# Norms and value copies moved to ScalarE, the output projection moved ahead of the next values, keys split around the rows' transposition: a four-layer cross-attention kernel with a mixture of experts

## The chip, the cores and the metric

The kernel runs on one core of one Trainium2 chip. The metric is the device time in microseconds (us) of one execution. Engines are named TensorE (PE in the profile, with its weight loads as PEld), VectorE (DVE), ScalarE (ACT), GpSimd (POOL) and SyncE (SP, which here only starts transfers).

## What is computed

The input is `x` (32 sequences of 128 positions, 256 wide) and a context of the same shape, all in fp32. Four layers follow each other, all with 16 heads of 16 dimensions:

```
L0: x = norm(x + attn(x -> ctx));  x = norm(x + relu(x W1) W2)         (key mask)
L1: x = norm(x + attn(x -> ctx))
L2: x = norm(x + attn(x -> x, causal) + bias);  x = norm(x + attn(x -> ctx));
    x = norm(x + top-2-of-8 mixture of experts(x))
L3: windowed attention, one shared key and value head; a silu gate;
    rms norm; the mean over the positions is subtracted
```

A layer norm is `(x - mean) * rsqrt(var + 1e-5) * g + b`. The causal attention has biases on queries, keys, values and output, and so has the cross attention of L2.

## The kernel before

The kernel has three stages. The **attention stage** (`slots`) handles L0, L1 and the two attentions of L2, which the code numbers `l` = 0 to 3. Its unit is a slot: one attention of one sequence. A round (`TPI`) is 16 slots, `tau` = 0 to 15: four layers for `NS` = 4 sequences, so `tau` 0 to 3 are `l` = 0 of four sequences, 4 to 7 are `l` = 1, and so on. Eight rounds make 128 slots; the first and last are unrolled by hand, the six between are a loop. The **expert stage** runs 71 tiles of 128 sorted rows through the experts. The **combine stage** (`cslots`, 32 slots) gathers the experts' results, norms them, and does L3.

Every engine has its own instruction stream, and the order inside a slot is written out by hand; semaphores (`wait`, `then_inc`) join the streams. An engine executes its stream in order, so whatever stands behind a waiting instruction waits too. Slot `now` is worked on together with its neighbours: `prev` (one before), `ff` (two before), `rk_` (three before), `nxt` (one after) and `nn` (two after). In a slot, in the order of each stream:

- TensorE: `scores(now)` into the four banks `ps_s`; the projections of queries and keys of `nxt` into `ps_qk` (`project_qk`); `av(prev)`, the attention-weighted values; `maxima_t`, which turns the row maxima round; `xt(nn)`, which turns the rows of `nn` round into the first half of bank `ps_xv`; `scores_t(now)`, the transposed scores minus the maxima; `values(nxt)` into the second half of `ps_xv`; `wo(prev)`, the output projection, into `ps_w`.
- VectorE: `norm_stats` (three small instructions), `maxima(now)` (L1520, one reduction over 128x2048), `norm_apply` (L1548, 128x256), `normalise(prev)` (the contexts are turned over by a 32x32 transposition out of PSUM, divided, and turned over again into `oT`, L1535), `vz_evac(nxt)` (the values are copied out of PSUM, with the bias added for `l` 2 and 3, L1489 and L1491), `qk_lo(nxt)` (the low parts of queries and keys), `residual_sum` (L1678, reads the output projection out of `ps_w`).
- ScalarE: `qk_evac(nxt)` (high parts of queries and keys out of `ps_qk`), `mt_evac` (copies the turned maxima into `mT`, which `scores_t` needs), `xt_evac(nn)`, `exps(now)` (four 128x512 exponentials), `fxt_evac` (rows for the feed-forward or the router).
- GpSimd: `root` (the inverse root of the variance, 128x1), `residual` (two 128x256 operations that need the norm's output), `expand` and `expand_lo` (queries spread over the heads), and in four slots of a round the two indirect stores of `scatter`.

The feed-forward of L0 makes slots 3 to 6 longer. A slot in which `rk_` is of layer 0 (`tau` 3 to 6) has `ff_output(rk_)` behind its scores, then `maxima_t`, `av`, for `tau` 3 to 5 `fxt(ff)`, `scores_t(now)`, `xt(nxt)` and `project(nxt)` (keys, values, queries), then `wo(prev)`; `tau` 6 has `xt(nxt)` and `project_qk` ahead of `scores_t`. Slots 2 to 5 end with `ff_hidden(ff)`, which fills `ps_xv` and `ps_qk`. VectorE applies two norms in the heavy slots, the one of `ff` and the one behind the feed-forward of `rk_`. In `tau` 14, 15, 0 and 1, `ff` is of layer 3 and `fxt(ff)` turns its rows round for the router, behind `wo`.

In the combine stage the maxima are turned round into the bank `ps_qk`, and `maxima_t` waits until the low parts of the slot after have been taken from that bank. There the norm is already applied by ScalarE (`combine_apply`, L1403), with the product of the negated mean and the inverse root made by GpSimd (`c_root`, L2103).

## Time and profile before

| | |
|---|---|
| median of 3 runs (lowest to highest) | 2236.9 us (2232.33 to 2238.15) |
| the profiled execution | 2241.2 us, span 2239.3 us |
| TensorE matmuls busy | 1964.6 us, 88% of the span |
| TensorE weight loads busy | 1664.2 us, 74% |
| VectorE busy | 1579.5 us, 71% |
| ScalarE busy | 1108.7 us, 50% |
| GpSimd busy | 1074.5 us, 48% |
| mean granted clock of TensorE | 0.972 of full speed |

The profile covers one execution. Each row below gives an instruction or a group of them with its line in the kernel (L1520 is line 1520), what it writes and reads (`out<-in`), its size and how many of them were merged. A time in square brackets is how long the engine stood still before it, and behind the arrow stands what ended that. Instructions of one engine overlap a little, so the next one can start before the one before it ends.

### The profile page before, as it was taken

Reading aid. Unit: us, or ns where it says so; the run is one execution under the profiler, and the core shown is the slowest. Engines: PE = TensorE matmul, PEld = TensorE weight load, DVE = VectorE, ACT = ScalarE, POOL = GpSimd, SP = SyncE. Lnnn points to the kernel's source line nnn. Section 1 sums busy time; section 2 is a strip of 40 time slices with the busy share of each in tenths; the row PEclk is TensorE's granted clock in tenths of the full one; section 3 lists DMA queues with packets and bytes.
Section 4 is the critical chain, followed back from the end, with each engine's and each line's share of the span. In section 5 each row is a group of like instructions: output and inputs, shape, how many; then the busy total and the mean of one; then the engine's idle time right before and its main releaser. Section 6 shows DMA issues by size and latency. Waiting matters only on the chain.

```text
span 2239.3 us, 72637 instructions
## 1 busy us (share of the span) xinstructions
PE 1964.6 (88%) x26040; PEld 1664.2 (74%) x26041; DVE 1579.5 (71%) x3469; ACT 1108.7 (50%) x2836; POOL 1074.5 (48%) x1432
## 2 busy tenths in 40 slices
PE   5988888888888888888888885999999996888887
PEld 4777777767767777777767764999999995666665
DVE  4688788787787787787787784544545454788886
ACT  2355355345354354354354442556565653566665
POOL 3455365465465464465454465140224004777874
PEclk9999999999999999999999996999999996999999
DMA  8401001001001001001000213121111112122120
GB/s 195 174 2 39 7 21 39 8 21 44 7 19 42 6 19 42 6 19 42 6 19 18 97 41 118 59 65 50 59 59 59 40 40 59 56 64 66 59 61 24
DMA packets 97540, 104.65 MB, mean 47 GB/s; under 512 B 23968, under 2 KB 88480, under 8 KB 97184
## 3 DMA queue, kind: packets, MB, share of 16 engines
q1 hardware_dynamic: 88224, 76.22, 11.4%
q0 software_dynamic: 8704, 25.19, 3.6%
q8 instruction: 167, 2.74, 0.5%
q14 instruction: 61, 0.50, 0.1%
q10 hardware_dynamic: 384, 0.01, 0.0%
HBM read 64.94 MB, written 36.44 MB: 45 GB/s over the span
## 4 chain that ended last, share of the span: by engine, by line
PE 48%; issue 20%; DVE 19%; POOL 6%; ACT 3%; DMA 1%; SPq 1%; another core or an unknown queue 1%; DVEq 1%; POOLq 0%; ACTq 0%
PE ps_scores L1106 11%; PE ps_w L1119 9%; DVE mb L1520 8%; PE ps_scores L880 5%; PE ps_xv L785 3%; PE ps_xv L707 3%; ACT pt_all L1272 3%; DVE lower L1508 3%; PE ps_scores L887 2%; PE ps_scores L860 2%; PE ps_qk L801 2%; PE ps_w L930 1%; POOL lower L1975 1%; POOL rstd L1991 1%; PE ps_scores L827 1%
## 5 line engine op out<-in xcount | busy, mean ns | idle before, releaser
L1520 DVE TENSOR_REDUCE mb<-ps_scores 128x16 bf16<-128x2048 f32 x160 | 365.8, 2286 | 57.3 <-PE ps_scores L860 56.4
L1272 ACT ACTIVATE pt_all<-ps_scores 128x512 f32<-128x512 f32 x512 | 267.1, 603 | 73.2 <-PE ps_scores L887 54.2
L1106 PEld LDWEIGHTS ps_scores<-tiles,w_now 128*128 128x128 f32 x2272 | 267.2, 193 | 4.8 <-issue 1.8
L1106 PE MATMUL ps_scores<-tiles,w_now 128*128 128x128 f32 x2272 | 267.8, 277 | 1.2 <-DVE tiles L1811 1.2
L1358 ACT ACTIVATE tiles<-ps_scores,b1s 128x128 f32<-128x128 f32 x568 | 154.2, 383 | 198.3 <-PE ps_scores L1106 182.8
L1991 POOL TENSOR_TENSOR rstd<-ve,neghalf 128x1 f32<-128x1 f32 x192 | 106.9, 557 | 280.5 <-DVE ve L1544 259.2
L1968 POOL TENSOR_TENSOR qbd_all<-qT,consts 128x512 fp32r<-128x512 f32 x160 | 177.6, 1110 | 97.9 <-ACT kT L1258 74.1
L1119 PE MATMUL ps_w<-w_split,g_split 128*128 x1136 | 219.4, 346 | 5.7 <-DVE g_split L1830 5.7
L1975 POOL TENSOR_TENSOR lower<-lower,consts 128x512 fp32r<-128x512 f32 x160 | 166.8, 1042 | 97.4 <-DVE lower L1508 63.0
L1119 PEld LDWEIGHTS ps_w<-w_split,g_split 128*128 128x128 f32 x1136 | 174.9, 190 | 30.4 <-issue 6.4
L917 PE MATMUL ps_o<-pt_all,vz 128*32 128x128 f32 x5120 | 175.4, 278 | 0.0
L1821 DVE TENSOR_TENSOR tiles<-ps_w,tiles 128x256 f32<-128x256 f32 x71 | 30.2, 425 | 186.8 <-PE ps_w L1119 186.8
L1243 ACT ACTIVATE xT<-ps_xv,cols_all 128x128 f32<-128x128 f32 x256 | 103.2, 453 | 115.2 <-PE ps_xv L707 114.2
L1996 POOL TENSOR_TENSOR xr<-xn,arena 128x256 f32<-128x256 f32 x128 | 92.9, 726 | 119.3 <-DVE xn L1548 119.3
L917 PEld LDWEIGHTS ps_o<-pt_all,vz 128*32 128x32 f32 x5120 | 131.7, 110 | 22.7 <-issue 13.8
L1261 ACT ACTIVATE qT<-ps_qk,cols_all 128x128 fp32r<-128x128 f32 x192 | 60.8, 373 | 173.6 <-PE ps_qk L801 173.6
L1350 ACT COPY w_now<-w_experts 128x2048 f32 x72 | 140.1, 1947 | 9.9 <-issue 9.9
L2094 POOL DMA_INDIRECT arena<-sorted_y,pidx x64 | 64.7, 1012 | 165.8 <-DMA sorted_y<-tiles 150.3
L2072 POOL CAST w_split<-w_raw 128x256 fp32r<-128x256 f32 x64 | 24.1, 420 | 243.7 <-DVE g_split L1830 238.2
L930 PE MATMUL ps_w<-arena,oT 128*128 128x256 f32 x512 | 135.8, 388 | 3.9 <-DVE oT L1535 3.0
L1532 DVE TENSOR_TENSOR route_all<-route_all,o_inv 128x256 f32<-128x256 f32 x160 | 130.5, 816 | 5.5
L707 PE MATMUL ps_xv<-consts,xn 128*128 128x128 f32 x384 | 79.9, 290 | 56.7 <-DVE xn L1548 37.0
(246 smaller groups left out, 4743.0 us busy)
## 6 DMA issues: line engine op xcount, KB each, us to landing
tiles<-sorted_x SPq DMA_DIRECT2D x72, 128.0 KB, 2.0
sorted_y<-tiles SPq DMA_DIRECT2D x71, 128.0 KB, 1.7
w_experts<-in_L_xattn_e_w SPq DMA_DIRECT2D x8, 1024.0 KB, 10.2
w_raw<-in_L_xattn_e_w POOLq DMA_DIRECT2D x8, 1024.0 KB
sorted_x<-zeros SPq DMA_DIRECT2D x8, 640.0 KB
ct_scratch<-cT SPq DMA_DIRECT2D x32, 128.0 KB, 1.7
x_scratch<-x2b_all SPq DMA_DIRECT2D x32, 128.0 KB, 1.7
arena<-x_scratch SPq DMA_DIRECT2D x32, 128.0 KB
```

The lines of the kernel that those rows point to most:

```text
L707: last = nc.tensor.transpose(ps[:, P * c:P * (c + 1)], src[:, P * c:P * (c + 1)], ident)
L917: last = mm(ps_o[32 * q:32 * q + 32, 2 * par + c, :], vz[p][:, h].rearrange("p a d -> p (a d)"), pt[:, SLOTS * q + PAIR * c + par, :], sta ...
L930: last = mm(ps_w[:, 0:D], oT[:, c, :], w[:, c, :], start=c == 0, stop=c == KC - 1)
L1106: last = mm(ps_s[:, 2 * par + j // 4, P * (j % 4):P * (j % 4 + 1)], w1_now[:, par, c, P * j:P * (j + 1)], xgT[par][:, c, :], start=c == 0, ...
L1119: return mm(ps_w[:, 0:n], g_split[:, g_, j, :].bitcast(F32R), w2_split[:, bass.ds(odd * (2 * FC * D) + j * 2 * D, n)].bitcast(F32R), start ...
L1272: nc.scalar.activation(pt[:, 4 * g:4 * g + 4, :].rearrange("p h q -> p (h q)"), ps_s[:, g, :], ACT.Exp, bias=bias, scale=LAYER[l]["scale"] ...
L1350: nc.scalar.copy(w1_now[:, par].rearrange("p c n -> p (c n)"), w1f[:, bass.ds(e * (KC * FF), KC * FF)]).then_inc(w1_copied, 1)
L1358: last = nc.scalar.activation(gT[:, j, :], ps_s[:, 2 * par + j // 4, P * (j % 4):P * (j % 4 + 1)], ACT.Gelu, bias=b1s[par][:, j:j + 1])
L1520: V.tensor_reduce(mb[:].rearrange("p (g r) -> p g r", g=BANKS)[:, :, 0:SLOTS], ps_s[:].rearrange("p g (h k) -> p g h k", h=SLOTS), AX_X, A ...
L1532: V.tensor_tensor(o_rows[:, 0].rearrange("p b (par d) -> p par b d", par=PAIR), o_rows[:, :, :, 0:HD], o_inv[:].unsqueeze(3).to_broadcast( ...
L1968: G.tensor_tensor(qbd[p].bitcast(F32R), qT[:].unsqueeze(2).to_broadcast([P, KC, PAIR, P]), hmask.unsqueeze(1).unsqueeze(3).to_broadcast([P ...
L1975: G.tensor_tensor(qbd_lo.bitcast(F32R), qT_lo.unsqueeze(2).to_broadcast([P, KC, PAIR, P]), hmask.unsqueeze(1).unsqueeze(3).to_broadcast([P ...
```

## The change

- Both layer norms of the attention stage are applied by ScalarE, as in the combine stage: VectorE makes a negated mean (`nm`), GpSimd the product with the inverse root (`nb`), ScalarE one activation with scale and bias (`norm_apply`, first in ScalarE's slot, or behind `mt_evac` in heavy slots).
- The values' copy moves from VectorE to ScalarE, behind the exponentials, except in slots whose `ff` is of layer 0. The value biases leave the copy: once, in the first round, they are multiplied by the output weights and added to the rows that the residual adds anyway.
- In light slots `wo(prev)` goes ahead of `values(nxt)`.
- In heavy slots the keys are made in halves, one ahead of and one behind `xt(nxt)`; in slot 6 `scores_t(now)` goes ahead of them; in slots 3 to 5 the second half of the keys is followed by values and queries as before.
- In the combine stage the maxima are turned round into the first half of `ps_xv` and wait for other things.

```diff
@@ TensorE
+        def maxima_t_c(n, ahead):
+            wait(pe, maxima_ready, n["t"] + 1)
+            wait(pe, xt_sb, n["t"] + ahead)
+            wait(pe, vz_ready, n["t"] + 1)
+            wait(pe, c_att_sb, n["b"] - 1)
+            nc.tensor.transpose(mt_bank_c, mb[:], ident_b[:]).then_inc(mt_psum, 1)
@@ heavy slots
                 maxima_t(now, t + 1)
+                if first and tau == NS + 1:
+                    ...
+                    for l, n_ in ((2, "L2_xattn_sa_bv"), (3, "L2_xattn_ca_bv")):
+                        for c in range(KC):
+                            last_ = mm(ps_o[:, 2 * (l - 2):2 * (l - 1), :].rearrange("p a b -> p (a b)"),
+                                       col[n_][:, c:c + 1].to_broadcast([P, P]), w_attn[l][3][:, c, :], start=c == 0, stop=c == KC - 1)
+                    last_.then_inc(bv_psum, 1)
+                    pe.wait_ge(bv_ready, 1)
                 av(prev)
...
                 if ff["l"] == 0:
                     fxt(ff, 2)
                     scores_t(now)
-                    xt(nxt, nxt["t"])
...
-                    project(nxt)
+                    wait(pe, mt_sb, nxt["t"])
+                    keys(nxt, (0,))
+                    xt(nxt, nxt["t"])
+                    keys(nxt, (1,))
+                    values(nxt, nxt["t"] + 1)
+                    queries(nxt)
                     wo(prev, False, w_free)
                 else:
+                    scores_t(now)
+                    wait(pe, mt_sb, nxt["t"])
+                    wait(pe, qk_lo_ready, nxt["t"])
+                    keys(nxt, (0,))
                     xt(nxt, nxt["t"])
-                    project_qk(nxt, nxt["t"])
-                    scores_t(now)
+                    keys(nxt, (1,))
+                    queries(nxt)
                     values(nxt, nxt["t"] + 1)
                     wo(prev, False, w_free)
@@ light slots
                     scores_t(now)
+                if prev["ok"]:
+                    wo(prev, first and tau - 1 == 0, w_free)
                 if nxt["ok"]:
...
                     values(nxt, nn["t"] + 1 if nn["ok"] and nn["l"] != 1 else nxt["t"] + 1)
-                if prev["ok"]:
-                    wo(prev, first and tau - 1 == 0, w_free)
@@ combine stage
-                maxima_t(now, now["t"] + (2 if nxt["ok"] else 1))
+                maxima_t_c(now, 2 if nxt["ok"] else 1)
@@ ScalarE
+        def norm_apply(kind, n, step, both, n_):
+            wait(act, both, n_ + 1)
+            nc.scalar.activation(xn[n["s"]][:], yb[kind][:], ACT.Identity, bias=nb[kind][:], scale=rstd[kind][:]).then_inc(step, 1)
...
             if ff_behind:
-                mt_evac(now, True)
+                mt_evac(now, mt_bank_ff)
+                norm_apply(0, ff, ln_step, rstd_ready, ff["t"])
                 if ff_now:
                     fxt_evac(ff, u_of(ff))
+                norm_apply(1, rk_, ffln_step, ffrstd_ready, rk_["j"] * NS + rk_["s"])
                 xt_evac(nxt)
...
             else:
+                if ff["ok"]:
+                    norm_apply(0, ff, ln_step, rstd_ready, ff["t"])
                 if nxt["ok"]:
                     qk_evac(nxt)
...
                 if now["ok"]:
                     exps(now)
+                if nxt["ok"] and not ff_now:
+                    wait(act, v_psum, nxt["t"] + 1)
+                    nc.scalar.copy(vz[nxt["p"]][:, :, 0, :], ps_xv[:, D:2 * D].rearrange("p (h d) -> p h d", d=HD)).then_inc(vz_ready, 1)
                 if ff["ok"] and ff["l"] == 3:
                     fxt_evac(ff, u_of(ff))
@@ VectorE
             V.tensor_scalar_add(ve[kind][:], mv[kind][:, 1:2], LN_EPS).then_inc(step, 1)
-        def norm_apply(kind, dst, y, step, rs_sem, n_):
-            wait(dve, rs_sem, n_ + 1)
-            V.tensor_scalar(dst, y, mv[kind][:, 0:1], rstd[kind][:], ALU.subtract, ALU.mult).then_inc(step, 1)
+            V.tensor_scalar_mul(nm[kind][:], mv[kind][:, 0:1], -1.0).then_inc(nm_done, 1)
...
                 if nxt["ok"]:
-                    vz_evac(nxt)
+                    if ff["ok"] and ff["l"] == 0:
+                        vz_evac(nxt)
@@ GpSimd
+        def root_and_mean(kind, step, n_, nm_done, done, both):
+            root(kind, step, 5 * n_ + 4, done)
+            wait(pool, nm_done, n_ + 1)
+            wait(pool, done, n_ + 1)
+            G.tensor_tensor(nb[kind][:], nm[kind][:], rstd[kind][:], ALU.mult).then_inc(both, 1)
```

## Rows read from the trace of the kernel before

**Rows 1.** Windows: busy us of each engine, then granted clock.

```profile
27.00:1345.00 1318.00, 1161.71 (x17402) 958.98 (x17403) 1044.75 (x2322) 599.46 (x1534) 691.27 (x848) 0.99 0.12 37
...
755.68:771.68 16.00, 13.23 (x143) 10.94 (x144) 11.01 (x32) 5.47 (x16) 6.06 (x8) 0.89 0.00 1
```

**Rows 2.** Timeline of VectorE in light slot 9.

```profile
788.75 2.29 DVE L1520 TENSOR_REDUCE mb<-ps_scores 128x16 bf16<-128x2048 f32 x1
790.96 0.40 DVE L1548 TENSOR_SCALAR xn<-yb,mv,rstd 128x256 f32<-128x256 f32 x1
...
793.30 0.45 DVE L1535 STREAM_TRANSPOSE oT<-route_all 128x256 f32<-128x256 f32 x1
794.36 0.42 DVE L1491 TENSOR_TENSOR vz<-ps_xv,arena 128x256 f32<-128x256 f32 x1 [0.61 <-PE ps_xv L785]
...
795.73 0.41 DVE L1678 TENSOR_TENSOR yb<-ps_w,xr 128x256 f32<-128x256 f32 x1
...
797.31 2.29 DVE L1520 TENSOR_REDUCE mb<-ps_scores 128x16 bf16<-128x2048 f32 x1
```

**Rows 3.** Timeline of TensorE in light slot 9.

```profile
791.18 0.23 PE L904 MATMUL ps_w<-ident_b,mb 128*128 128x128 bf16 x1 [0.65 <-DVE mb L1520]
...
793.19 1.13 PE L785 MATMUL ps_xv<-arena,xT 128*128 128x256 f32 x4
794.15 1.03 PE L930 MATMUL ps_w<-arena,oT 128*128 128x256 f32 x4
795.41 0.40 PE L827 MATMUL ps_scores<-ident_b,route_all 32*128 32x128 bf16 x16 [0.23 <-ACT pt_all L1272]
...
799.74 0.23 PE L904 MATMUL ps_w<-ident_b,mb 128*128 128x128 bf16 x1 [0.70 <-DVE mb L1520]
```

**Rows 4.** Timeline of ScalarE and GpSimd in slot 9.

```profile
793.29 2.06 ACT L1272 ACTIVATE pt_all<-ps_scores 128x512 f32<-128x512 f32 x4 [0.52 <-PE ps_scores L887]
...
791.44 0.73 POOL L1996 TENSOR_TENSOR xr<-xn,arena 128x256 f32<-128x256 f32 x1 [1.75 <-DVE xn L1548]
...
797.68 0.57 POOL L1991 TENSOR_TENSOR rstd<-ve,neghalf 128x1 f32<-128x1 f32 x1
```

**Rows 5.** Groups by line, combine stage: busy us, mean ns.

```profile
L2103 POOL TENSOR_TENSOR c_nb<-c_nm,rstd 128x1 f32<-128x1 f32 x30 | 5.7, 190 | 2.4
...
L1403 ACT ACTIVATE xn<-yb,c_nb,rstd 128x256 f32<-128x256 f32 x31 | 19.1, 617 | 1.4 <-POOL c_nb L2103 1.4
...
L1428 ACT COPY arena<-ps_w 128x256 f32<-128x256 f32 x30 | 11.9, 398 | 8.4 <-PE ps_w L930 8.4
```

**Rows 6.** Timeline of VectorE in heavy slot 12.

```profile
814.24 2.28 DVE L1520 TENSOR_REDUCE mb<-ps_scores 128x16 bf16<-128x2048 f32 x1
...
822.57 2.28 DVE L1520 TENSOR_REDUCE mb<-ps_scores 128x16 bf16<-128x2048 f32 x1
```

**Rows 7.** Timeline of TensorE in slots 1 and 2.

```profile
696.06 0.38 PE L707 MATMUL ps_xv<-consts,xn 128*128 128x128 f32 x2
696.91 0.40 PE L834 MATMUL ps_scores<-x2b_all,ecol_b 32*128 32x512 bf16 x4 [0.46 <-ACT pt_all L1272]
...
703.89 1.95 PE L951 MATMUL ps_xv<-fxT,arena 128*128 128x128 f32 x16
```

**Rows 8.** Timeline of TensorE and VectorE in slot 5.

```profile
739.21 3.72 PE L964 MATMUL ps_w<-arena 128*128 128x256 f32 x16
...
746.58 0.43 PE L707 MATMUL ps_xv<-consts,xn 128*128 128x128 f32 x2 [1.07 <-DVE xn L1548]
...
743.46 0.42 DVE L1714 TENSOR_TENSOR yb<-ps_w,xr 128x256 f32<-128x256 f32 x1
```

**Rows 9.** Timeline of TensorE in slot 6.

```profile
762.86 0.44 PE L707 MATMUL ps_xv<-consts,xn 128*128 128x128 f32 x2 [2.11 <-DVE xn L1548]
```

**Rows 10.** Timeline of TensorE and VectorE in the combine stage.

```profile
2030.41 0.22 PE L899 MATMUL ps_qk<-ident_b,mb 128*128 128x128 bf16 x1 [1.05 <-DVE lower L1503]
...
2032.64 0.39 DVE L1889 TENSOR_TENSOR arena<-ps_w,row_L_xattn_bg 128x256 f32<-128x256 f32 x1
```

More of the change, by code:

```diff
@@ L302, in program @@
     c_nm, c_nb = sb("c_nm", [1]), sb("c_nb", [1])
+    nm, nb = [sb(f"nm{i}", [1]) for i in range(2)], [sb(f"nb{i}", [1]) for i in range(2)]
     tt = sb("tt", [8, E])
@@ L726, in xt @@
                 wait(pe, c_att_sb, n["b"] - 3)
+                wait(pe, mt_sb, n["t"] - 1)
                 transposes(ps_xv, xn[n["s"]], xt_psum)
@@ L755, in attn_loaded, with keys @@
                 pe.wait_ge(ld_ca, 16 * 4)
-        def keys(n):
+        def keys(n, halves=range(KC)):
             l = n["l"]
@@ L764, in keys @@
             else:
-                for o in range(KC):
+                for o in halves:
                     for c in range(KC):
@@ L802, in queries @@
             last.then_inc(qk_psum, 1)
-        def project(n):
-            wait(pe, mt_sb, n["t"])
-            if n["l"] != 0:
-                keys(n)
-            values(n, n["t"] + 1)
-            queries(n)
         def project_qk(n, maxima):
@@ L971, in router @@
                 wait(pe, ln_step, 5 * (t + 1) + 1)
+            else:
+                wait(pe, rt_lg, n["j"] * NS + n["s"])
             for c in range(KC):
@@ L1262, in qk_evac, with mt_evac @@
             last.then_inc(qk_sb, 1)
-        def mt_evac(n, with_qk):
+        def mt_evac(n, bank):
             wait(act, mt_psum, n["t"] + 1)
-            nc.scalar.copy(mT[:], mt_bank(with_qk)).then_inc(mt_sb, 1)
+            nc.scalar.copy(mT[:], bank).then_inc(mt_sb, 1)
         def exps(n, groups=range(4)):
@@ L1325, in run @@
                 if now["ok"]:
-                    mt_evac(now, False)
+                    mt_evac(now, mt_bank_light)
                 if nn["ok"] and nn["l"] != 1:
@@ L1440, in run_c @@
             if now["ok"]:
-                mt_evac(now, True)
+                mt_evac(now, mt_bank_c)
             if nn["ok"]:
@@ L1667, in run @@
                     wait(dve, scattered[now["s"]], 32 * now["j"])
+            if first and tau == NS + 1:
+                dve.wait_ge(bv_psum, 1)
+                for l, n_ in ((2, "L1_xattn_beta"), (3, "L2_xattn_ln1_b")):
+                    last_ = V.tensor_tensor(rows[n_], rows[n_], ps_o[:, 2 * (l - 2):2 * (l - 1), :].rearrange("p a b -> p (a b)"), ALU.add)
+                last_.then_inc(bv_ready, 1)
             if ff["ok"] and ff_slot:
-                norm_stats(0, yb[0][:], ln_step, ff["t"])
+                norm_stats(0, yb[0][:], ln_step, ff["t"], ln_nm)
             if routing:
@@ L2030, in run @@
             if ff_behind:
-                root(1, ffln_step, 5 * f + 4, ffrstd_ready)
+                root_and_mean(1, ffln_step, f, ffln_nm, ffroot_done, ffrstd_ready)
+            if first and tau == NS + 2:
+                pool.wait_ge(bv_ready, 1)
             if ff["ok"]:
```

55 lines of the change are left out of this document (27 added, 28 removed).

## Prediction

> **What bounds the kernel now.** I read the stages first, then one slot of each kind engine by engine, then the waits. The attention stage, 128 slots from 27 to 1345 us, is 1318 of the span's 2239.3 us; its matmuls are busy 88% of it and VectorE 79% [rows 1], so neither is the bound all the time and the slots have to be read one by one. A round is 16 slots, numbered 0 to 15 as `tau` in the code; slots 3 to 6 carry a feed-forward (heavy), the others do not (light). I measure a slot from maxima (L1520) to maxima.
>
> A light slot is a ring through VectorE. In slot 9 maxima start at 788.75 and again at 797.31: 8.56 us. Between them VectorE applies a norm (0.40), turns the contexts (oT done at 793.75), stands still 0.61 for the values, copies them, makes the low parts, and adds the residual only at 795.73 [rows 2], although TensorE's output projection, begun at 794.15, was over at 795.18 [rows 3]. TensorE in turn stands 0.65 to 0.70 for the maxima and 0.23 for the exponentials [rows 3]. So in the light slots VectorE's queue is the bound, by 0.7 us. In heavy slots it is TensorE, with one hole: it waits 1.07 us for the second norm in slot 5 [rows 8] and 2.11 us in slot 6 [rows 9].
>
> **The change, part by part.** I call E the end of the maxima (791.04 in slot 9).
>
> *Light slot, VectorE.* Without the norm oT comes 0.3 to 0.4 us earlier, 0.33 taken: E+2.4. The projection no longer has the values ahead of it: it could start when they did, 793.19 = E+2.15, and now waits for oT until E+2.45; its 1.03 us [rows 3] end at E+3.5. The values' copy leaves VectorE: from its start at 794.36 to the residual at 795.73 are 1.37 us [rows 2], less some 0.34 for the copy, so the low parts are done at E+3.45 and the residual starts at E+3.6 (0.13 after the projection). From there to the next maxima it was 1.58 us [rows 2]; the new negated mean (128x1) adds 0.07 to 0.15. Ring: 3.6 + 1.65 + 2.29 = 7.55 us.
>
> *Light slot, TensorE.* From 791.18 to 799.74 are 8.56 us, of which 0.93 idle [rows 3]: 7.63 of work. The exponentials begin at 793.29 and take 2.06 [rows 4], and the next scores can only start at 795.41, 2.22 after the transposed scores ended; projection and values fill 1.92 of that, 0.30 stays a wait. TensorE's ring is 7.9 us and becomes the bound in the masked slots 8 to 11: 0.66 saved each, 2.6. Slots 7, 12 and 13 lack one or both mask passes (some 0.2 us each); slot 12 takes 8.33 [rows 6] and falls to VectorE's 7.55: 0.75 each, 2.25.
>
> *The norm's new way.* GpSimd's product is 0.19 us and the activation 0.617 where this kernel already does both [rows 5]; VectorE's norm is 0.40 [rows 2]. The way from the variance to the norm's end is then 0.08 + 0.55 + 0.08 + 0.19 + 0.04 + 0.61 = 1.55 us against some 1.1. In light slots this is covered: the maxima run for 2.29 meanwhile. If the cover were gone, 0.45 a slot would come back. Behind the norm in ScalarE's queue stand the evacuation of queries and keys (some 1.15) and then mT, for which TensorE waits: 1.55 + 1.15 = 2.7 us after the variance, which is just when the maxima and their transposition are over (2.29 + 0.4). I cost it at nothing. GpSimd's queue in the scatter slots 7 to 10: from the residual (791.44) to the next root (797.68) are 6.24 us [rows 4], plus root, product and norm 1.5: 7.75, still under 7.9.
>
> *Slots 14, 15, 0 and 1* have a router transposition (`fxt`) that waits for the values' copy. This was on VectorE at once; now it is behind the exponentials. In slot 1 `fxt` ran at 696.06 and the scores at 696.91, when the exponentials were done [rows 7]. Now: copy 0.40 (a PSUM copy of that size, [rows 5]), then `fxt` 0.3, then scores: 0.7 later, of which VectorE had 0.3 in hand. Slot 1 loses 0.35, slot 0 breaks even, slots 14 and 15, limited by VectorE like slot 12, still gain 0.45 each. Net 0.55 saved.
>
> *Slot 2* ends in `ff_hidden`, which began at 703.89 [rows 7] and needs the bank free of the values. It started when the projection had been issued, the values long copied. The projection, which hangs on oT, moves 0.33 forward to 703.55, but now the values (0.71) and VectorE's copy of them (0.42, with 0.2 for the two hand-overs) come behind it: 704.9. That is on TensorE's path: 1.0 lost.
>
> *Heavy slots.* In slot 5 the feed-forward's sum was taken at 743.46 because VectorE first waited for the other norm [rows 8]; the matmuls it needs end at 742.93 [rows 8], so it moves 0.4 forward. The norm's way is 0.45 longer, but the old one ran at 0.80 instead of 0.40 beside GpSimd's work, so these cancel: the rows' transposition moves from 746.58 to about 746.2. The first half of the keys fills the hole before it, but the values still need the rows' evacuation 1.33 us behind it, so the slot gains 0.4, not 1.07. Slots 3 and 4: 0.4 each. Slot 5 also had TensorE waiting for VectorE behind router work: 0.75. In slot 6 the 2.11 us hole [rows 9] is filled by the transposed scores (1.2): 1.2 saved.
>
> *Combine stage.* The transposed maxima wait 1.05 us for the low parts at 2030.41 [rows 10] and no longer would. But the exponentials there stand behind the gate's tanh, and the gate's sum is on VectorE at 2032.64 [rows 10], after work that this edit does not move. Bounds: nothing, or up to 0.8 in some 28 slots, 22 us. I take nothing, since the tanh follows that sum at once.
>
> *One-off.* Folding the value biases into rows costs eight matmul passes, two sums and two waits in the first round: 3 us.
>
> **Sum.** Per round 2.6 + 2.25 + 0.55 - 1.0 + 0.4 + 0.4 + 0.75 + 1.2 = 7.15 us; eight rounds 57, less 3: 54 to 55. The profiled execution took 2241.2 (span 2239.3), 4.3 above the median of the runs shown, 2236.9. So 2241.2 - 55 = 2186 for a profiled one, and **2182** for a median.
>
> The Trainium skill speaks against the move: "ScalarE: Activation LUTs", Rules for kernel authors, has additions and multiplications done on VectorE, not ScalarE. The rows agree on the cost of one (0.617 against 0.40); whether it counts is a matter of cover, and by the rule alone the sum would be the second rival's.
>
> **The rivals.** (1) *The slower engine is on the path.* A norm costs 0.21 more on ScalarE, 160 times 34 us: 2216. For it: ScalarE's queue is in order and mT stands behind norm and evacuation with no slack in my count. Against: ScalarE is busy only 45% of the stage [rows 1]. The rule above is this rival. (2) *The combine stage's wait was real and the clock helps.* Slot 6 took 16.00 us at a mean granted clock of 0.89 [rows 1], after TensorE's hole of 2.11; fewer holes may spare such stretches, 5 to 8 us in all, and up to 22 us come from the combine stage: 2158. (3) *Slower: mT waits for the norm.* If variance to mT takes 1.4 us longer than my 2.7 (slower hops to GpSimd and back, product as dear as a root), TensorE idles in every light slot. The gain of 0.66 is used up at 3.4 us; at 4.1 each of 88 light slots loses 0.7 against my sum plus what it saved: 2182 + 88 x 0.8 = 2252. (4) *No change*: TensorE, 88% busy, takes new waits for oT where it lost old ones, and slots 1, 2, 14, 15 cost double: 2234 to 2240.
>
> **How the numbers follow.** Chances: forecast 0.58 (2160 to 2203), slower engine 0.17, combine and clock 0.12, no change 0.05, slower 0.08. Faster by over 0.3%, about what a measurement here can tell, is 0.87; within it 0.05; slower 0.08. The range goes from 2158 (rival 2) to 2222 (rival 1 and a little).
>
> **What would show it.** Right: slots 8 to 11 near 7.9 us with a wait of about 0.3 for exponentials and none for the maxima; slots 12, 13 near 7.5; slot 2 near 11.4 with VectorE's value copy ahead of `ff_hidden`; slot 1 longer; slot 6's wait for the norm gone; combine slots unchanged. Wrong: mT late behind qT and kT on ScalarE; GpSimd's root late in slots 7 to 10; the projection waiting over 0.5 us for oT; combine slots shorter by over 0.3 us.

## The result, and the profile after

The changed kernel takes 2244.7 us (median of 20 runs, 2235.3 to 2249.6) against 2236.5 (20 runs, 2226.3 to 2241.2): a ratio of 1.0035, 95% interval 1.0023 to 1.0047. The forecast was 2182. The profiled execution took 2237.9 (span 2233.1), 6.8 below its median, and that of before 4.7 above its own, so spans show a gain of 6 us where medians show a loss of 8. A second profile (after_again, below) has the same slots with longer stretches at the lower clock. Stages and slots are what can be read from them.

The two long stages, by windows from maxima to maxima (busy time of each engine, then granted clock). First after: the attention stage, the combine stage and slot 0 of round 4; then the two stages of before, cut the same way:

```profile
24.98:1362.37 1337.39, 1169.40 (x17337) 964.97 (x17336) 956.97 (x2231) 717.36 (x1776) 710.04 (x1004) 0.98 0.12 36
1908.86:2216.00 307.14, 286.79 (x4873) 227.53 (x4872) 260.56 (x572) 204.64 (x613) 252.38 (x334) 0.98 0.20 61
690.83:702.82 11.99, 8.41 (x120) 6.88 (x121) 6.29 (x15) 5.41 (x13) 5.69 (x9) 0.86 0.07 23
```

```profile
27.09:1339.91 1312.82, 1158.77 (x17332) 956.65 (x17336) 1040.23 (x2315) 598.43 (x1531) 689.00 (x845) 0.99 0.12 37
1886.79:2222.30 335.51, 286.78 (x4873) 227.64 (x4872) 264.40 (x572) 207.85 (x614) 253.62 (x334) 0.97 0.19 55
```

The attention stage grew from 1312.8 to 1337.4 us, and the combine stage (to its last maxima 326.9 before, 298.7 after) shrank by 28. I had forecast -55 and 0. Slots of the attention stage in us, from maxima to maxima, means of rounds 2 to 6; "forecast" and "measured" are changes from before, and the last three columns are runs told of below. The slot-15 mean includes the way out of the loop in round 6 (10.79 before, 12.19 after; in most other rounds 8.25 and 9.18):

```
slot     before  after  forecast  measured | no scatter  pad24  final_mix
0          8.69  12.57      0       +3.88  |   12.47      8.48     7.93
1          7.83   8.35    +0.35     +0.52  |    8.32      8.32     7.82
2         10.43  11.06    +1.0      +0.63  |   11.06     11.61    10.42
3 + 4     31.09  30.35    -0.8      -0.74  |   30.34     30.35    30.35
5         16.35  15.18    -0.75     -1.17  |   15.18     15.18    15.18
6         15.22  13.71    -1.2      -1.51  |   13.71     13.71    13.65
7          8.55   7.86    -0.75     -0.69  |    7.82      7.82     7.75
8          8.55   9.18    -0.66     +0.63  |    7.83      9.35     7.80
9          8.55   9.83    -0.66     +1.28  |    8.19     10.23     7.79
10         8.53   9.99    -0.66     +1.46  |    7.82     10.90     7.81
11         8.46   7.82    -0.66     -0.64  |    7.83      8.03     7.76
12 + 13   16.50  15.65    -1.5      -0.85  |   15.65     15.64    15.50
14         8.57   8.40    -0.45     -0.17  |    8.41      8.41     8.55
15         9.02   9.79    -0.45     +0.77  |    9.77      9.17     8.11
round    166.33 169.74    -7.15     +3.41  |  164.39    167.20   156.43
```

Two places miss by far: slots 8 to 10 and slot 0. Slot 9 of round 3, timeline of TensorE, ScalarE, GpSimd and VectorE:

```profile
633.07 0.41 PE L888 MATMUL ps_scores<-mT,ecol_b 32*128 32x128 bf16 x16
633.66 1.13 PE L939 MATMUL ps_w<-arena,oT 128*128 128x256 f32 x4 [0.17 <-DVE oT L1572]
634.62 1.03 PE L793 MATMUL ps_xv<-arena,xT 128*128 128x256 f32 x4
637.94 0.40 PE L828 MATMUL ps_scores<-ident_b,route_all 32*128 32x128 bf16 x16 [2.29 <-ACT pt_all L1303]
...
635.82 2.07 ACT L1303 ACTIVATE pt_all<-ps_scores 128x512 f32<-128x512 f32 x4 [3.04 <-remote]
...
633.01 1.05 POOL L2048 DMA_INDIRECT sorted_x<-x2b_all,posu  x1 [0.17 <-issue]
634.37 0.97 POOL L2048 DMA_INDIRECT sorted_x<-x2b_all,posu  x1 [0.30 <-issue]
635.98 1.04 POOL L2012 TENSOR_TENSOR lower<-lower,consts 128x512 fp32r<-128x512 f32 x1 [0.64 <-remote]
...
636.43 0.42 DVE L1717 TENSOR_TENSOR yb<-ps_w,xr 128x256 f32<-128x256 f32 x1 [1.83 <-PE ps_w L939]
```

The transposed scores (L888) end at 633.48 and the projection (L939) at 634.79, by the records. Yet the exponentials, which wait for the first, start at 635.82 (their wait is put down to "remote": no instruction ended near), and the residual, which waits for the second, at 636.43. In slot 9 of before the exponentials follow the scores at once [rows 4]. What differs is when the engines are told. The trace also has the time of each update of a semaphore: those of L888 came at 635.80, of L939 at 635.96, of the values at 636.02. GpSimd issued its two indirect DMAs (the scatter of rows into `sorted_x`) at 633.01 and 634.37. TensorE then stands still for 2.29 us.

Between the two kernels it is above all the pair that moved. Counted from the start of the maxima, in slots 7 to 10 of rounds 2 to 6, the pair begins at 5.57 to 5.59 us before, 1.0 to 1.3 behind the end of the transposed scores; after, mostly at 4.39 to 4.43, while the scores mostly end at 4.31 to 4.87. On ScalarE the norm no longer waits behind the maxima on VectorE, so GpSimd's residual starts earlier: 1.31 us behind the start of the maxima in the slot above, 2.69 in slot 9 of before.

Slot 0, timeline of TensorE at the head of round 2; the first four rows are after, the three of the second fence the same place of run pad24:

```profile
350.54 0.40 PE L835 MATMUL ps_scores<-kmask,ecol_b 32*128 32x512 bf16 x4 [0.64 <-issue]
350.77 0.40 PE L861 MATMUL ps_scores<-kT,qbd_all 32*128 32x128 bf16 x16
353.23 1.21 PE L804 MATMUL ps_qk<-xT,arena 128*128 128x128 f32 x4 [2.06 <-issue]
...
355.88 1.94 PE L926 MATMUL ps_o<-pt_all,vz 128*32 128x128 f32 x32
```

```profile
350.41 0.40 PE L835 MATMUL ps_scores<-kmask,ecol_b 32*128 32x512 bf16 x4 [0.74 <-issue]
350.63 0.40 PE L861 MATMUL ps_scores<-kT,qbd_all 32*128 32x128 bf16 x16
350.96 0.71 PE L804 MATMUL ps_qk<-xT,arena 128*128 128x128 f32 x4
```

TensorE stands still for 2.06 us for nothing that the profile shows ("issue"), 45 instructions past the head of its loop, and then works at half the clock (1.2 in place of 2.4 GHz): the contexts (L926) take 1.94 us, 1.08 otherwise. The trace names a clock of 0.5 for 3.4 or 6.8 us behind this place in each of rounds 2 to 6, and the window of slot 0 of round 4 above has a mean of 0.86.

Groups by line, attention stage after: ScalarE's exponentials without the key mask, norm and copy of the values, then TensorE's rows that wait for the copy or for oT (busy, mean ns, idle before and its releaser):

```profile
L1303 ACT ACTIVATE pt_all<-ps_scores 128x512 f32<-128x512 f32 x380 | 196.2, 606 | 78.7 <-remote 48.5 <-PE ps_scores L888 30.2
L1316 ACT ACTIVATE xn<-yb,nb,rstd 128x256 f32<-128x256 f32 x157 | 94.2, 600 | 113.1 <-POOL nb L2035 112.3
...
L1375 ACT COPY vz<-ps_xv 128x256 f32<-128x256 f32 x87 | 33.2, 382 | 22.3 <-PE ps_xv L793 17.6 <-PE ps_xv L787 2.2 <-issue 1.3
...
L939 PE MATMUL ps_w<-arena,oT 128*128 128x256 f32 x504 | 139.3, 399 | 39.4 <-DVE oT L1572 39.2
...
L714 PE MATMUL ps_xv<-consts,xn 128*128 128x128 f32 x314 | 64.8, 288 | 31.2 <-ACT vz L1375 14.3 <-DVE ve L1581 5.2 <-ACT xn L1316 3.6
```

48.5 us of the exponentials' waiting have no releaser; [rows 3] had TensorE wait for the maxima in each light slot, now it waits for oT, 39.2 us in all.

Slot 12, timeline of VectorE and TensorE, which shows what bounds a light slot now:

```profile
657.60 2.28 DVE L1557 TENSOR_REDUCE mb<-ps_scores 128x16 bf16<-128x2048 f32 x1
660.35 0.72 DVE L1565 STREAM_TRANSPOSE route_all<-ps_o 128x512 f32<-128x512 f32 x1 [0.47 <-PE ps_o L926]
...
661.39 0.73 DVE L1569 TENSOR_TENSOR route_all<-route_all,o_inv 128x256 f32<-128x256 f32 x1
662.16 0.45 DVE L1572 STREAM_TRANSPOSE oT<-route_all 128x256 f32<-128x256 f32 x1
...
663.92 0.42 DVE L1717 TENSOR_TENSOR yb<-ps_w,xr 128x256 f32<-128x256 f32 x1 [0.31 <-PE ps_w L939]
...
659.13 1.08 PE L926 MATMUL ps_o<-pt_all,vz 128*32 128x128 f32 x32
660.14 0.23 PE L913 MATMUL ps_w<-ident_b,mb 128*128 128x128 bf16 x1
...
662.66 1.13 PE L939 MATMUL ps_w<-arena,oT 128*128 128x256 f32 x4 [0.71 <-DVE oT L1572]
663.63 1.03 PE L793 MATMUL ps_xv<-arena,cT 128*128 128x256 f32 x4
664.59 0.41 PE L861 MATMUL ps_scores<-kT,qbd_all 32*128 32x128 bf16 x16
```

TensorE has 7.1 us of work and waits 0.71 for oT, which comes at E+2.73, not the E+2.4 that I took: the contexts are only there at 660.21 (E+0.33), and the scaling (L1569) takes 0.73. The slot is 7.83.

Combine stage, timeline of before (TensorE, GpSimd, ScalarE) and then of after:

```profile
2032.70 0.40 PE L887 MATMUL ps_scores<-mT,ecol_b 32*128 32x128 bf16 x16
...
2033.00 1.04 POOL L2094 DMA_INDIRECT arena<-sorted_y,pidx  x1 [0.16 <-issue]
2034.34 0.95 POOL L2094 DMA_INDIRECT arena<-sorted_y,pidx  x1 [0.30 <-issue]
...
2034.37 2.31 ACT L1272 ACTIVATE pt_all<-ps_scores 128x512 f32<-128x512 f32 x4 [0.89 <-PE ps_scores L887]
```

```profile
2052.30 0.41 PE L888 MATMUL ps_scores<-mT,ecol_b 32*128 32x128 bf16 x16
...
2053.41 1.03 POOL L2140 DMA_INDIRECT arena<-sorted_y,pidx  x1 [0.17 <-issue]
2054.76 0.96 POOL L2140 DMA_INDIRECT arena<-sorted_y,pidx  x1 [0.32 <-issue]
...
2053.81 2.04 ACT L1303 ACTIVATE pt_all<-ps_scores 128x512 f32<-128x512 f32 x4
```

Before, the transposed scores ended at 2033.10, just behind the start of a gather's indirect DMA, and their semaphore was updated only at 2034.35 (one slot later 2.66 us late); the exponentials start then, not behind the tanh, which was done at 2033.48. After, the scores end at 2052.71, ahead of the gather.

### The profile page after: what moved, and what is told of

Its sections match the earlier page's. It is cut to its first block, busy times and chain, and to the rows that moved or that the text cites. A ratio compares the mean times of both kernels' runs of the same rounds, so it can differ in the third digit from the quotient of the medians.

```text
span 2233.1 us, 73195 instructions
## 1 busy us (share of the span) xinstructions
PE 1975.6 (88%) x26048; PEld 1672.5 (75%) x26049; DVE 1491.8 (67%) x3384; ACT 1226.0 (55%) x3083; POOL 1094.3 (49%) x1592
## 4 chain that ended last, share of the span: by engine, by line
PE 65%; DVE 14%; issue 9%; ACT 5%; another core or an unknown queue 2%; POOL 2%; DMA 0%; DVEq 0%; ACTq 0%; POOLq 0%; SPq 0%
PE ps_scores L1137 11%; PE ps_w L1150 9%; PE ps_w L939 6%; PE ps_qk L809 5%; PE ps_o L926 5%; DVE mb L1557 4%; PE ps_qk L775 4%; PE ps_xv L714 3%; PE ps_xv L793 3%; PE ps_scores L881 3%; PE ps_qk L960 3%; PE ps_xv L960 3%; ACT pt_all L1303 3%; DVE route_all L1569 2%
## 5 line engine op out<-in xcount | busy, mean ns | idle before, releaser
L2005 POOL TENSOR_TENSOR qbd_all<-qT,consts 128x512 fp32r<-128x512 f32 x160 | 167.5, 1047 | 104.4 <-ACT kT L1289 79.9
L926 PE MATMUL ps_o<-pt_all,vz 128*32 128x128 f32 x5120 | 179.2, 282 | 0.8 <-DVE arena L1705 0.8
L939 PE MATMUL ps_w<-arena,oT 128*128 128x256 f32 x512 | 142.5, 401 | 41.5 <-DVE oT L1572 41.3
L1316 ACT ACTIVATE xn<-yb,nb,rstd 128x256 f32<-128x256 f32 x160 | 96.0, 600 | 114.8 <-POOL nb L2035 114.0
L926 PEld LDWEIGHTS ps_o<-pt_all,vz 128*32 128x32 f32 x5120 | 134.4, 112 | 24.2 <-issue 13.6
L1565 DVE STREAM_TRANSPOSE route_all<-ps_o 128x512 f32<-128x512 f32 x160 | 114.3, 715 | 52.0 <-PE ps_o L926 49.9
L939 PEld LDWEIGHTS ps_w<-arena,oT 128*128 128x128 f32 x512 | 87.9, 190 | 65.3 <-DVE oT L1572 56.9
L1569 DVE TENSOR_TENSOR route_all<-route_all,o_inv 128x256 f32<-128x256 f32 x160 | 115.9, 724 | 5.5
```

Source lines behind the costliest of these rows:

```text
L926: last = mm(ps_o[32 * q:32 * q + 32, 2 * par + c, :], vz[p][:, h].rearrange("p a d -> p (a d)"), pt[:, SLOTS * q + PAIR * c + par, :], sta ...
L939: last = mm(ps_w[:, 0:D], oT[:, c, :], w[:, c, :], start=c == 0, stop=c == KC - 1)
L1569: V.tensor_tensor(o_rows[:, 0].rearrange("p b (par d) -> p par b d", par=PAIR), o_rows[:, :, :, 0:HD], o_inv[:].unsqueeze(3).to_broadcast( ...
L2005: G.tensor_tensor(qbd[p].bitcast(F32R), qT[:].unsqueeze(2).to_broadcast([P, KC, PAIR, P]), hmask.unsqueeze(1).unsqueeze(3).to_broadcast([P ...
```

## The experiments

Each run was timed against the kernel before on the same chip, and the ratios are to that (before = 1). There were four sittings: on chip 3 (the two runs without scatter, after_pad24; the kernel before took 2234.7 us), on chip 7 (both runs in which GpSimd waits, before_combine_bank, after_again; 2236.3) and twice on chip 9 (the runs called best_, 2223.9; after_direct, before_pad24 and final_mix, 2222.0).

**The chips differ in the very thing looked for.** The latest update of a TensorE semaphore, in us, rounds 1 to 7 of the attention stage and then the combine stage, in which every one of these kernels gathers with pairs of indirect DMAs:

```
                                      attention   combine
before (chip not on record)              1.48       2.70
after (the same)                         2.35       1.95
after_no_scatter, chip 3                 0.05       2.03
before_no_scatter, chip 3                0.05       2.70
after_pad24, chip 3                      2.42       2.31
after_again, chip 7                      2.35       1.95
the two with GpSimd's wait, chip 7       1.17       1.96
before_combine_bank, chip 7              1.44       1.93
all seven of chip 9                 0.06 to 0.21   0.05 to 0.15
```

On chip 9 nothing is late by more than 0.21 us, not even in before_pad24, whose pairs of indirect DMAs stand where those of the kernel before do. So no run of chip 9 says anything on what makes signals late, and its runs are not to be set against times of chip 7. Whether it is the chip or the hour, no run tells.

**No scatter** (after_no_scatter, before_no_scatter). In `scatter`, GpSimd's indirect DMA is replaced by a bare increment of its semaphore.

```
-                G.indirect_dma_start(sorted_x, bass.IndirectOffsetOnAxis(posu4[:, s, k_:k_ + 1], 0),
-                                     x2b[s], None).then_inc(scattered[s], 16)
+                pool.sem_inc(scattered[s], 16)
```

> The changed kernel without GpSimd's indirect DMAs that scatter rows into sorted_x in the attention stage (left out: the scatter, and the experts read rows of zeros instead). Theory A, TensorE's signals are held up while a pair of indirect DMAs is issued: slots 8, 9 and 10 of rounds 1 to 7 fall from 9.1 to 9.9 us to about 7.8, as they are in round 0, which scatters nothing; 22 slots save some 1.8 us each, 40 us, to about 2205. Theory B, ScalarE or GpSimd is simply too full in those slots: then the 2.3 us of issue that GpSimd loses would matter but ScalarE's wait for the scores would stay, and slots 8 to 10 end near 8.5 to 9. Theory C, the round's first slot causes the loss: these slots stay at 11.4 us in either case.

> The kernel before with the same scatter left out. Theory A: its signals are held up too (1.2 us at the scores), but under VectorE's work, so slots 7 to 10 keep their 8.5 us and the time moves by under 5 us. Theory B: GpSimd is relieved in both kernels, so this one gains too, 0.3 us or more a slot in 32 slots, 10 us.

Measured: 2194.2 us, 0.982 [0.979, 0.986], by the ratios 47 us less than the changed kernel; in the traces 42 of it are in the attention stage and 5 in the expert stage, which reads one fixed block of rows here. Slots 8 and 10 are at 7.83 and 7.82, slot 9 at 8.19 (table), slot 0 is all but unchanged. In the attention stage no update of TensorE's is late by over 0.06 us, while in the combine stage of the same execution, whose gathers are as they were, updates are up to 2.03 late. The kernel before without the scatter: 0.998 [0.996, 1.000]. Theory A; in the kernel before the updates of the scores (L860) are 1.0 to 1.5 us late, but VectorE was busy meanwhile. The line of the exponentials in the run without scatter:

```profile
L1303 ACT ACTIVATE pt_all<-ps_scores 128x512 f32<-128x512 f32 x384 | 198.3, 605 | 39.8 <-PE ps_scores L888 39.8
```

**Plain DMAs** (after_direct): the same bytes from the same queue, without offsets from a tile.

```
-                G.indirect_dma_start(sorted_x, ...)
+                pool.dma_start(sorted_x[bass.ds(((n["j"] * NS + s) * TOPK + k_) * P, P), :], x2b[s]).then_inc(scattered[s], 16)
```

> The changed kernel with GpSimd's two indirect DMAs of a slot replaced by two plain DMAs of the same bytes from the same queue to fixed places (left out: the sorting; the experts read rows of zeros). Theory A, the indirect form (its offsets and descriptors, written by GpSimd) holds the signals: none is late by over 0.3 us, slots 8 to 10 take 7.8 us as without the scatter, near 2195. Theory B, the packets of the transfer do it: signals stay late by 0.5 to 2.3 us and the slots at 9 to 10 us, near 2245.

Measured: 2185.0, 0.983 [0.981, 0.985]; slots 8 to 10 at 7.83, 8.20, 7.84, the numbers that theory A stated. It decides nothing: this is a run of chip 9, and in its combine stage, where the indirect gathers are untouched, no update is late by over 0.13 us either (on chips 3 and 7 up to 2.31). Whether the indirect form or the traffic holds the signals is open.

**GpSimd waits** (after_scatter_waits2): the pair is issued behind the slot's transposed scores. Without the condition on `now` (after_scatter_waits) the program stands still for ever, since the last slots have no scores to wait for; it gave no time.

```
+                    if now["ok"]:
+                        wait(pool, st_ready, 4 * (now["t"] + 1))
                     scatter(routed(at_, 8 + s), s)
```

> The changed kernel, and GpSimd waits for the transposed scores' signal of its slot (where there is one) before it issues the pair of indirect DMAs. Theory A: the signal on which the exponentials hang is then ahead of the pair, so slots 8 to 10 fall from 9.1 to 9.9 us to 7.9 to 8.6; 20 to 35 us less than the changed kernel, 2210 to 2225. Theory B, GpSimd's queue is only made later: slots 7 to 10 grow by 0.5 each, 14 us slower.

Measured: 2209.8, 0.987 [0.984, 0.991], 36 us less than the changed kernel by the ratios, 42 less than after_again in the same sitting; slots 8 to 10 at 8.58, 8.59, 8.56, slot 7 at 8.41 (7.86), slot 11 at 7.36. The pair now begins 5.44 to 5.71 us behind the start of the maxima, behind the scores, and the scores' updates (L888) are on time. The slots are at the top of the stated band; slot 7 is 0.55 longer, and the gain of the other three is larger.

**The loop's head** (after_pad24, before_pad24): 24 matmuls of 128x1, some 48 instructions, ahead of everything.

```
+                for _ in range(24):
+                    mm(ps_o[:, 0, 0:1], ident, ident[:, 0:1], start=True, stop=True)
                 xt(now, 0)
```

> The changed kernel with 24 small matmuls (128x1) into an unused bank at TensorE's start, so that the round's loop begins at another place of its instruction stream. Theory A, the 2.7 us in which TensorE stands still for nothing that the profile shows at the head of rounds 2 to 7 is the fetching of code behind the jump, and how much of the body is at hand depends on where it begins: slot 0 falls from 12 to 13 us to under 10, and the stretches at the lower clock behind it go; 15 to 20 us less. Theory B, the stall is a wait of the work itself: no slot moves by over 0.2 us.

> The kernel before with the same 24 small matmuls ahead. The stall at the loop's head is 1.3 us there, with VectorE the bound: if it is the place of the loop in the code, slot 0 changes from 8.2 to 8.5 us to between 7.9 and 9.5, under 8 us in all either way. If the time moves by over 10 us, the place of the code matters at other jumps too.

Measured: 2225.1, 0.996 [0.995, 0.998]: 48 more instructions in the program make it some 16 us faster by the ratios (1.0035 to 0.996). Slot 0 is 8.48 in place of 12.57, at the full clock in five rounds of five. Slots 8 to 10 still have their late updates and are even longer, by 1.5 us in the three, and slot 2 is by 0.55. In the kernel before 0.998 [0.996, 1.000]: its stall was 1.3 to 1.6 us long and 63 instructions past the head, mostly beside VectorE's work; with the padding it is gone from there, and TensorE is idle 0.9 to 1.4 us ahead of the round's first matmuls (L834) instead.

**Both** (pad24_scatter_waits).

> The 24 small matmuls ahead of the loop and GpSimd's wait together. If the head of the round and the held signals are two causes that have nothing to do with each other, the savings add: some 20 and some 20 to 35, to 2190 to 2205. If one was only hiding behind the other, about the better one of the two alone.

Measured: 2196.2, 0.983 [0.979, 0.986]. Two causes, and they nearly add: by the ratios 16 and 36 us by themselves, 47 together (55 less than after_again in the same sitting).

**The combine part alone** (before_combine_bank): the kernel before with `mt_bank_c`, `maxima_t_c` and the wait in `xt`, and nothing else.

> The kernel before with one part of the change: in the combine stage the transposed maxima go through the bank of the values, and so wait no longer for the low parts. Theory A: the transposed scores' signal then is ahead of the gathers' indirect DMAs, the exponentials follow at once, and combine slots fall from 10.0 to 11.5 us to about 9.5, 28 us in all, to about 2208. Theory B, the combine stage gains through the attention stage's other state or the norms: nothing here.

Measured: 2207.8, 0.987 [0.984, 0.991], attention stage within 1 us, most combine slots 9.4 to 9.6. The edit that I costed at nothing is worth 28 us. It does not show that late signals were what it saved. Chip 9 has kernels with the old and the new bank in the combine stage and no late update in either: before_pad24 has combine slots of mostly 10.02 to 10.09 and a stage of 315.1 us, after_direct 9.17 to 9.31 and 290.6. So some 24 us come without any late signal (the two differ in the attention stage too); where signals are late the stages take 326.9 and 298.7, a gain of 28. A slot of before_pad24:

```profile
1981.28 0.22 PE L899 MATMUL ps_qk<-ident_b,mb 128*128 128x128 bf16 x1 [1.09 <-DVE lower L1505]
1983.57 0.40 PE L887 MATMUL ps_scores<-mT,ecol_b 32*128 32x128 bf16 x16
...
1983.82 1.04 POOL L2096 DMA_INDIRECT arena<-sorted_y,pidx  x1 [0.16 <-issue]
1983.88 0.42 ACT L1450 ACTIVATE arena<-arena 128x256 f32<-128x256 f32 x1
1984.20 2.04 ACT L1274 ACTIVATE pt_all<-ps_scores 128x512 f32<-128x512 f32 x4
```

Here the exponentials do follow the tanh (L1450), as I had it. But TensorE, once its 1.09 us for the low parts are over, shows no further wait up to the next maxima at 1988.10: it is the bound, and its wait is what the edit takes away.

**The changed kernel again** (after_again).

> The changed kernel once more, as it is, for a second profile. The profile shown was of a short execution (2237.9 against a median of 2244.7). Expected: slots 8 to 10 again 9 to 11 us in rounds 1 to 7, slot 0 again 12 to 13, and what differs is how long the stretches at the lower clock are, some 7 us in all.

Measured: 2251.3, 1.006 [1.004, 1.008] (profiled: 2241.8). Slots 8 to 10 at 9.27, 10.16, 10.42, slot 0 at 13.20; the stretch at half clock behind the loop's head is 6.8 us long in rounds 2 to 7, all six, where the first profile has it so in four and 3.4 us in two. The profile is as expected, and the median is 7 us above that of the first measurement.

**Undoing parts**, each from pad24_scatter_waits (0.983, but on chip 7, while these are runs of chip 9, so total times are not set against it). The attention stages can be compared with some care: slots 7 to 11 together take 41.4 us in pad24_scatter_waits and in best_vz_split, which has the same code there. That stage takes 1288.7 us in pad24_scatter_waits, 1296.9, 1283.2, 1300.2 and 1299.9 in the four. best_norm_vector has both norms on VectorE again; best_values_first exchanges `wo` and `values` in the light slots; best_vz_split gives the copy back to VectorE in slots 0, 1, 14 and 15 (`ff["l"] in (0, 3)` in place of `ff["l"] == 0`); best_mix adds the values first in slot 2.

> From the same kernel: both norms back on VectorE, without the negated mean and GpSimd's product. Theory A, the norm on ScalarE is what relieved VectorE's ring in the light slots: slots 8 to 14 rise by 0.2 to 0.4 us, slots 3 to 6 by 0.3 or nothing, 20 to 30 us slower, about 2220. Theory B, the slower engine cost as much as it gave: within 8 us of 2196.

Measured: 0.985 [0.982, 0.987], nearer to theory B: slots 3 to 6 are 2.9 us longer in each round, slots 8 to 10 are 2.4 shorter (7.8; that GpSimd's and ScalarE's queues are shorter there is not shown to be the reason), slots 7 and 11 are 0.9 and 0.4 longer, 12 and 13 the same within 0.1. With GpSimd's wait in place the move of the norm pays in the heavy slots; in slots 7 to 11 it costs 1.1 us in the five.

> From the same kernel: the values again ahead of the output projection in the light slots. Theory A, the new order is what lets the residual start early: slots 7 to 13 rise by 0.5 us or more, slots 1, 2 and 15 fall by 0.5 (no wait for oT, and ff_hidden starts earlier); in sum 15 to 25 us slower. Theory B, it only trades the wait for the values against a wait for oT (0.45 to 0.7 us): within 8 us.

Measured: 0.980 [0.977, 0.983], theory B: slots 12 and 13 rise by 0.07 only, slot 2 falls by 1.0. Slot 11 rises by 1.2 and slots 7 and 10 fall by 0.5 and 0.4; a round is 0.1 us shorter in all. The order by itself is worth nothing that can be told here.

> From the padded kernel with GpSimd's wait (2196.2 us, slots 14, 15, 0, 1 of 8.4, 9.3, 8.4, 8.3 us): the values' copy goes back to VectorE in the slots where the router's transposition waits for it (0, 1, 14, 15). Theory A, the copy behind the exponentials costs TensorE its wait there (0.41 to 0.55 us): those four slots lose 0.3 to 0.9 us each, 10 to 18 us in all, to about 2182. Theory B, VectorE is as full as TensorE there, and the copy's 0.4 us come back on it: no change.

Measured: 0.990 [0.987, 0.994], an attention stage 11.5 us longer: both theories missed. Slot 14 rises from 8.40 to 10.33. Its timeline on VectorE:

```profile
664.34 0.45 DVE L1574 STREAM_TRANSPOSE oT<-route_all 128x256 f32<-128x256 f32 x1
666.87 0.42 DVE L1531 COPY vz<-ps_xv 128x256 f32<-128x256 f32 x1 [2.09 <-PE ps_xv L793]
667.21 0.60 DVE L1547 SCALAR_TENSOR_TENSOR lower<-ps_qk,cols_all,qT 128x128 fp32r<-128x128 f32 x2
```

The values now come behind the projection, which waits for oT, and the copy stands ahead of the low parts and the residual in VectorE's queue: 2.09 us idle. In slot 14, then, order and engine of the copy hang together: with the projection first the copy is better ScalarE's. Slots 15, 0 and 1 moved by 0.3 or less.

> The kernel with the split copy, and in slot 2 alone the values ahead of the projection, since ff_hidden there waits for their copy. Expected on top of the split copy: slot 2 from 11.6 us back to some 10.4 to 10.8, 7 to 9 us less, about 2175. If slot 2's length is set by the projection or VectorE instead, nothing.

Measured: 0.986 [0.984, 0.989]; slot 2 falls from 10.86 to 9.91, 7.6 us in eight rounds as stated, but slot 15 rises from 9.15 to 10.09, for which I have no cause (in best_vz_split it is 8.4 to 8.6 in some rounds and 10.1 in others, here 9.9 to 10.1 in all but the first); the stage is as long as without it.

**What each part is good for, put together** (final_mix): padding and GpSimd's wait; norms on ScalarE in slots 3 to 6, on VectorE in the others; in slots 0, 1, 2, 14 and 15 values first and copied by VectorE, elsewhere projection first and ScalarE.

```
+                hidden_next = ff["ok"] and ff["l"] in (0, 3)
+                if prev["ok"] and not hidden_next:
                     wo(prev, first and tau - 1 == 0, w_free)
...
                     values(nxt, ...)
+                if prev["ok"] and hidden_next:
+                    wo(prev, False, w_free)
```

> The padded kernel with GpSimd's wait, the norm on ScalarE in the heavy slots 3 to 6 and on VectorE in the light ones; in slots 0, 1, 2, 14 and 15 the values ahead of the projection and copied by VectorE, as in the kernel before. If each slot keeps what it showed by itself: slots 3 to 6 as the changed kernel (59.4 us, against 61.8 with the norms on VectorE), 8 to 10 at 7.8, 2 at 9.9 to 10.4, 14 and 15 at 8.4: 0.972 to 0.978 of the kernel before. If norms that change their engine between slots bring new waits, about 0.982 as the best so far.

Measured: 2142.2 against 2222.0, 0.963 [0.961, 0.966], 80 us less than the kernel before and better than the stated band. A round is 156.43 us. That no update is late by over 0.2 us is no merit of this kernel: it is so in every run of chip 9. How it does where signals are late wasn't tried. Its attention stage by windows:

```profile
24.98:1271.20 1246.22, 1146.91 (x17337) 948.08 (x17336) 991.79 (x2258) 656.18 (x1655) 699.33 (x909) 1.00 0.13 39
```

The clock is full throughout, and the stage takes 1246.2 us, 67 less than in the profile of before; I had forecast 54 to 55 for it from the changed kernel. A part of the 67 belongs to the chip and the execution: the spans differ by 97 us where the medians differ by 80.

## Why the prediction was wrong

The forecast was 2182 us and the changed kernel took 2244.7. Two things that the sum had at nothing took the gain, the place of GpSimd's pair of indirect DMAs and the place of the loop's head; a third term at nothing, the combine stage, was a gain.

The rival nearest in time, "no change", named new waits for oT and a doubled cost of slots 1, 2, 14 and 15; those waits are there, but they are not what took the gain.

- *GpSimd's queue in the scatter slots.* "7.75, still under 7.9" counted the two indirect DMAs as 2.3 us of GpSimd's own time. It is not what failed: slots 7 and 11 are as forecast, and 8 to 10 without the scatter are 7.83, 8.19, 7.82. What failed is the idea that such an instruction costs nobody else anything, wherever in the slot it stands. The sum priced the length of GpSimd's queue and not the place of the pair, which came 1.2 us earlier with the norm and so stood at the end of the transposed scores: 5.35 us a round off forecast, in 7 rounds. Shown on chip 3 by taking the scatter away and on chip 7 by making it wait; on both chips a kernel that leaves the pair where it was has the late updates (after_pad24, after_again).
- *Slot 0, "breaks even".* The steps that I listed for it came out nearly (8.48 in the padded run against 8.69 before, in four of its five rounds 8.2 to 8.5; slot 1 +0.52 against +0.35). What the sum left out, at nothing and without a word, is that an edit moves TensorE's code: the stall near the loop's head grew from 1.3 to 1.6 us to 2.1 to 2.65 and went from beside VectorE's work onto the path: +3.9 us in rounds 2 to 6. That it hangs on the place of the code is shown by padding.
- *Combine stage, "I take nothing".* Bound given, 22 us; measured 28, shown by before_combine_bank. The step that failed is that the exponentials, standing behind the gate's tanh, close the slot: they do stand there (before_pad24, above), and the edit still gives 0.85 us a slot, since TensorE's wait of 1.05 us for the low parts was real, as rival 2 had it. The rest, a few us, is late signals: in the slot of [rows 10] the exponentials began 0.89 us behind the tanh, with a releaser that had ended long before, which I read past.
- *Slots 14 and 15*: -0.9 forecast, +0.6 measured. I had let them gain like slot 12 and took only a little off for the later copy; no run undoes that step by itself. With the old order, the old engine of copy and norm (final_mix) slot 15 is at 8.11, slot 14 at 8.55. *Slots 12 and 13*: 7.8, not 7.55, since oT comes at E+2.73.
- Right: slots 3 to 7 and 11 (-4.2 forecast, -4.75 measured, slot 6's hole filled), slot 2's sign and size (+0.63 in the changed kernel, +1.2 in the padded one, against +1.0), slot 1, the norm's cost (0.600 measured, 0.617 taken). The "slower engine" rival, and with it the Trainium skill's rule of "ScalarE: Activation LUTs", Rules for kernel authors, that arithmetic belongs on VectorE, is half borne out: with GpSimd's wait the norm is better on VectorE by 1.1 us in slots 7 to 11 together, and in the heavy slots better on ScalarE by 0.7 us each. (The prediction calls this the second rival's sum in one place; it is rival 1.)
- The sum: 10.56 us a round between forecast and measurement; 5.35 of it slots 8 to 10, 3.88 slot 0, 1.5 slots 14 and 15, 0.65 slots 12 and 13, and 0.8 the other way. Against it the combine stage's 28 us: without them the miss of the median would have been larger by as much.

## What to carry to other kernels

A signal's time is not its instruction's end: where a wait has no releaser or one that ended long before, compare the semaphore's updates with the instructions' ends, and look at what GpSimd issues there. A shift of a microsecond can move such a pair of DMAs onto a critical signal, with the sign of the change hanging on it, so place them behind the signals that matter, not where their own queue has room. Before an experiment is said to have removed something, look in a part of the same trace that it left alone: if it is gone there too, the place of the run removed it and not the edit. And before a change in a looped program is judged, look at the idle time at the loop's head: here it belonged to the code's place, and in the changed kernel padding took it away.

## What the runs showed of the hardware

**Updates of semaphores around a pair of indirect DMAs from GpSimd** (the second starts 1.36 us behind the first). When a signal of TensorE was due by its instruction's end, and how late its update came, in slots 7 to 10 of rounds 1 to 7 of before and after:

```
due, us after the start of          late by, us
the first:   -0.22 to -0.04         0.00 to 0.02   (after, L888)
              0.06 to  0.09         0.47 to 0.50   (after, L888)
              0.26 to  0.28         1.73 to 1.78   (after, L888)
              0.40 to  0.48         2.25 to 2.35   (after, L888)
              0.65 to  0.96         0.01 to 0.02   (before, L930)
the second:   0.06 to  0.56         1.02 to 1.48   (before, L860)
              0.85 to  0.88         0.71 to 0.74   (after, L888)
              1.27 to  1.29         0.01 to 0.37   (after, L793)
              2.04 and later        0.01 to 0.05   (before)
```

What was held is let go at about 0.56, 2.0 or 2.75 us behind the first's start, or 1.6 behind the second's. The projection's signals (L939), due 0.33 to 0.42 behind the second, came 0.95 to 1.18 late, but in a few slots within 0.22. Only TensorE's signals are in this table. Why signals due 0.65 to 0.96 behind the first pass, and what in the chip holds the others, stays open. Whether a single indirect DMA or a plain one does it wasn't tried where signals are late.

The same signals are on time on chip 9. In the combine stage of eleven traces with the new bank, the four signals of L888 fall due 0.30 to 0.34 us behind a first DMA in one slot: they are 1.68 to 1.77 us late in six of them (after and five runs of chips 3 and 7) and 0.00 to 0.01 in the five of chip 9. L861 of the attention stage, due 1.72 to 1.74 behind the first with GpSimd's wait, is 1.1 late on chip 7 and 0.02 to 0.03 on chip 9 (best_vz_split, best_mix).

**The loop's head.** In the changed kernel TensorE stands still 2.1 to 2.65 us, 45 instructions past the head, in each of rounds 2 to 6, on chips 3, 7 and 9 as well (slot 0 at 12.5 to 13.2 in all of them); 63 instructions and 1.3 to 1.6 us in the kernel before; nothing there in the changed kernel with 48 instructions more ahead. The Trainium skill, "Runtime: NRT & Kernel Launch", Instruction fetch mechanics, says that code is fetched in blocks of 16 KiB and that a taken branch out of what is held forces a fetch before execution goes on. The trace agrees on the size: a packet of instructions of 16384 bytes begins at 350.73 in round 2 and takes 1.01 us. That the standing still is the wait for it is not shown: the packet is over at 351.74 and TensorE goes on only at 353.04, and the padded kernel has the same packet (350.52, 0.95 us) and no such wait.
